# A transformer kernel on one NeuronCore: the key transposes placed ahead of the scores in each group of short TensorE steps

## Chip, cores and metric

The kernel runs on one core of one Trainium2 chip, as a single program. The metric is the device time of one execution in microseconds (us), lower is better.

## What is computed

Two layers of a perceiver-like model over 8 samples of 32 tokens, with a context of 512 rows of 512 numbers for each sample. Each layer has a cross attention, a second token mixer and a feed-forward part. The change touches the cross attention, which both layers have. Cut to what matters (layer 0; layer 1 has no latent keys, so 512 keys rather than 544, and adds a mask):

```python
kv = jnp.concatenate([context, latents], axis=1)
q = (latents @ Wq).reshape(bsz, q_len, HEADS, HEAD_DIM).transpose(0, 2, 1, 3)
k = (kv @ Wk).reshape(bsz, kv_len, KV_HEADS, HEAD_DIM).transpose(0, 2, 1, 3)
v = (kv @ Wv).reshape(bsz, kv_len, KV_HEADS, HEAD_DIM).transpose(0, 2, 1, 3)
q = rms_norm(q, q_norm_w)
k = rms_norm(k, k_norm_w)
scores = jnp.einsum('bhgqd,bhkd->bhgqk', qg, k) * scale
probs = jax.nn.softmax(scores.astype(jnp.float32), axis=-1).astype(q.dtype)
out = jnp.einsum('bhgqk,bhkd->bhgqd', probs, v)
return out @ Wo
```

There are 32 query heads and 8 key heads of 128, so four query heads of 32 tokens (128 rows) share one key head.

## The kernel before

**Tiling.** A unit is one sample with four of the eight key heads (`UNIT_H`); there are 16 units in a layer (`UNITS`). A unit's keys and values are made from its context in two quads, `side` 0 and 1, so there are 32 quads in a layer (`PAIRS`), numbered `m = 2 * u + side`. A quad makes two key tiles (`kn`, each 128 keys by four heads) and two value tiles by seven half-size products of 6 matmuls (p1 to p7, line 1736, run by `mm3`, lines 54 to 56). Each product is in a split form: three matmuls for one, of a rounded part and a rest.

**A key tile's way.** ScalarE copies a product to `kn` (line 1947 for the tile of parity 0, 1997 for parity 1), VectorE adds the other product to tile 0 (2126), ScalarE squares (1928), VectorE sums the squares (2101), GpSimd takes the root (1674, 1677), VectorE multiplies `kn` by it (2107: "normalise", it increments `k_normed`). Then TensorE transposes the tile in four steps to the bank `g_ktbank` (`kt`, lines 1794 to 1800), ScalarE takes the rounded part to `kT_hi` (1896) and VectorE the rest (2052, it increments `kt_lo`).

**A head's way.** `score` (lines 1741 to 1761): the head's queries against the four transposed key tiles, into the bank `g_sbank`; three matmuls of 512 columns in layer 1, six of 272 in layer 0. VectorE takes the maximum (2070 in layer 0, 2075 in layer 1), ScalarE the exponential (1909), VectorE the inverse of the sum (2061), ScalarE scales (1916). `p_transpose` (1763 to 1773) transposes the result `p` to `g_pobanks` in four steps, with one more for the latent keys in layer 0 (1769). ScalarE copies it to `pT` (1923), and `pv` (1775 to 1792) multiplies with the values, 8 recorded matmuls, in layer 0 with one more for the latent keys (1790, whose operand VectorE makes in lines 2084 to 2087).

**Order.** Nothing schedules the program: each engine's list is written out by hand, and engines wait for each other's semaphores. TensorE's list for a quad is `quad` in lines 1802 to 1858. Between the products stand two groups of short steps. The first (lines 1829 to 1833) comes after p2, and transposes the key tile of parity 1 of the quad before, `kt(2 * m - 1, 1)`; the second (1846 to 1850) comes after p5's place in the list, and transposes the tile of parity 0 of this quad, `kt(2 * m, 0)`. In each group the transposes of one head's `p`, the scores of a later head and the values' product of the first stand around it. In quads 0 to 2 (`early`) the first tile is transposed later, and in unit 0 the second one.

GpSimd's list for a quad (1705 to 1720) takes the root for the tile of the quad before; on side 1 the split of the next queries follows directly (`split_queries`, 1688 and 1692).

Of the kernel before, what the change touches and what calls it, by code (L numbers as in the profile page):

```python
# [44 lines left out]
def need(eng, sem, value):  # L45

    if isinstance(value, int) and value <= 0:
        return
    eng.wait_ge(sem, value)


def mm3(nc, out, a, b, start, stop, reopen=False):

    nc.tensor.matmul(out, a[0], b[1], start=start, stop=False, skip_group_check=reopen)  # L54
    nc.tensor.matmul(out, a[0], b[0], start=False, stop=False, skip_group_check=reopen)  # L55
    return nc.tensor.matmul(out, a[1], b[0], start=False, stop=stop, skip_group_check=reopen)  # L56
# [272 lines left out]
def is_at(i, value):  # L329

    return isinstance(i, int) and i == value
# [1083 lines left out]
def attend(layer, ctx, banks, border, follow=None, then=None):  # L1415
# [95 lines left out]
    def kept(m, name):  # L1511

        return len(COPIES) * m + COPIES.index(name) + 1

    def prepared(hf, m):

        return tail and hf == 0 and not is_at(m, PAIRS // 2)
# [26 lines left out]
    def early(m):  # L1544

        return is_at(m, 0) or is_at(m, 1) or is_at(m, 2)

    def exists(a):

        return not isinstance(a, int) or 0 <= a < UNIT_H * UNITS  # L1550

    def scored(u, par, side, second):

        if second:
            return UNIT_H * (u - 1) + 2 * side, u - 1, 1 - par, 2 * side
        if side:
            return UNIT_H * (u - 1) + 1, u - 1, 1 - par, 1
        return UNIT_H * (u - 2) + 3, u - 2, par, 3

    def summed_up(u, par, side, second):  # L1560

        if side:
            return UNIT_H * (u - 1) + int(second), u - 1, 1 - par, int(second)
        return UNIT_H * (u - 2) + 2 + int(second), u - 2, par, 2 + int(second)
# [166 lines left out]
    def tensor(pe):  # L1731
        def product(hf, side, left, right, bank, start):

            a, wt = context.block(side, left), kvw.block(hf, right)
            for c in range(DC // 2):
                last = mm3(nc, bank[:, :], tuple(h[:, c * P:(c + 1) * P] for h in a),
                           tuple(h[:, c * UW:(c + 1) * UW] for h in wt),
                           start and c == 0, c == DC // 2 - 1, not start)
            return last

        def score(a, u, apar, k):

            if not exists(a):
                return
            if k == 0:
                pe.wait_ge(kt_lo, CT * (u + 1))
                pe.wait_ge(q_lo, u + 1)
                if tail:
                    pe.wait_ge(kl_lo, u + 1)
            if tail:  # L1750
                need(pe, p_ready, a)
                for qp, kp in ((0, 1), (0, 0), (1, 0)):
                    for side in range(2):
                        last = nc.tensor.matmul(sbank[:, side * CTX:side * CTX + HALF], q[qp][:, apar, k, :],  # L1754
                                                kT[kp][:, apar, k, side * HALF:(side + 1) * HALF],
                                                start=(kp == 1), stop=(qp == 1))
            else:
                need(pe, m_done, a)
                last = mm3(nc, sbank[:, 0:CTX], tuple(h[:, apar, k, :] for h in q),
                           tuple(h[:, apar, k, :] for h in kT), True, True)  # L1760
            last.then_inc(s_done, 1)

        def p_transpose(a, free, value, bank):
            if not exists(a):
                return
            pe.wait_ge(p_scaled, a + 1)
            if tail:
                pe.wait_ge(free, value)
                nc.tensor.transpose(bank[0:SEQ, 0:P], p[:, CTX:KEYS], ident[:]).then_inc(tail_turned, 1)
            need(pe, pt_ready, a)  # L1770
            for t in range(CT):
                last = nc.tensor.transpose(ptbank[:, t * P:(t + 1) * P], p[:, t * P:(t + 1) * P], ident[:])  # L1772
            last.then_inc(pt_done, 1)

        def pv(a, u, apar, k, loads):

            if not exists(a):
                return
            if k == 0:
                pe.wait_ge(va_added, 2 * (u + 1))  # L1780
                if tail:
                    pe.wait_ge(vlat_loaded[apar], loads)
            pe.wait_ge(pt_ready, a + 1)
            need(pe, ot_ready, a)
            for t in range(CT):
                last = nc.tensor.matmul(obank[:, 0:P], v[:, apar, t, k * HD:(k + 1) * HD], pT[:, t, :],  # L1786
                                        start=(t == 0), stop=(t == CT - 1 and not tail))
            if tail:
                pe.wait_ge(tail_ready, a + 1)
                last = nc.tensor.matmul(obank[:, 0:P], vlat[:, apar, k * HD:(k + 1) * HD], pTs[:, :],  # L1790
                                        start=False, stop=True)
            last.then_inc(o_done, 1)

        def kt(n, k):
            pe.wait_ge(k_normed, n + 1)
            need(pe, kt_lo, n)
            for h in range(UNIT_H):
                last = nc.tensor.transpose(ktbank[:, h * P:(h + 1) * P],  # L1798
                                           kn[:, k, h * P:(h + 1) * P], ident[:])
            last.then_inc(kt_done, 1)  # L1800

        def quad(hf, j, b, par, cycle, u, side, m):
            x_bank, y_bank = kbank[side], kbank[1 - side]
            fresh = (is_at(u, 0) or is_at(u, TURN)) and side == 0
            loads = 48 * (cycle + par)

            def wait_context(i):
                if prepared(hf, m):
                    pe.wait_ge(context.lo_ready, 2 * m + i + 1)
                else:  # L1810
                    pe.wait_ge(context.fetched[side][i], 16 * (u - (TURN if tail else 0)) + 16)

            def wait_weights(i):
                if fresh:
                    kvw.wait_block(pe, hf, i)

            wait_context(0)
            wait_weights(kvw.B11)
            need(pe, ka_added, m)
            product(hf, side, context.A11, kvw.B11, x_bank, True).then_inc(products, 1)  # L1820
            if is_at(m, 0):
                border.turn(pe, 0)
            wait_weights(kvw.B21)
            need(pe, copied, len(COPIES) * m)
            product(hf, side, context.A12, kvw.B21, y_bank, True).then_inc(products, 1)
            if is_at(m, 0):
                border.turn(pe, 1)
            else:
                p_transpose(summed_up(u, par, side, False)[0], va_added, m, zbank)
                score(*scored(u, par, side, False))  # L1830
                if not early(m):
                    kt(2 * m - 1, 1)
                pv(*summed_up(u, par, side, False), loads)
            wait_weights(kvw.T2)
            pe.wait_ge(copied, kept(m, "p1"))
            product(hf, side, context.S2, kvw.T2, x_bank, False).then_inc(products, 1)
            if early(m) and not is_at(m, 0):
                kt(2 * m - 1, 1)
            wait_context(1)
            wait_weights(kvw.T1)  # L1840
            need(pe, va_added, m)
            product(hf, side, context.S1, kvw.T1, zbank, True).then_inc(products, 1)
            wait_weights(kvw.T3)
            pe.wait_ge(copied, kept(m, "u2"))
            product(hf, side, context.S3, kvw.T3, x_bank, False).then_inc(products, 1)
            p_transpose(summed_up(u, par, side, True)[0], ka_added, m + 1, y_bank)
            score(*scored(u, par, side, True))
            if not is_at(u, 0):
                kt(2 * m, 0)
            pv(*summed_up(u, par, side, True), loads)  # L1850
            wait_weights(kvw.T4)
            pe.wait_ge(copied, kept(m, "u3"))
            product(hf, side, context.A22, kvw.T4, x_bank, False).then_inc(products, 1)
            if is_at(u, 0):
                kt(2 * m, 0)
            wait_weights(kvw.B22)
            pe.wait_ge(vb_added, m + 1)
            product(hf, side, context.S4, kvw.B22, zbank, False).then_inc(products, 1)
# [1570 lines left out]
```

## Time and profile before

| What | Value |
|---|---|
| Median of 3 runs | 1445.07 us (1444.0 to 1445.44) |
| The profiled execution's own time | 1443.81 us |
| Its span in the profile | 1442.0 us |
| TensorE matmul busy | 1414.9 us (98%) |
| TensorE weight load busy (beside the matmuls) | 1193.5 us (83%) |
| VectorE busy | 1021.4 us (71%) |
| ScalarE busy | 844.8 us (59%) |
| GpSimd busy | 361.7 us (25%) |
| Mean granted TensorE clock | 0.999 of full speed |

The profile is of one execution. Its own time is 1.81 us over its span, which covers first to last instruction. Matmuls are pipelined: a record lasts longer than the step from it to the next, so that the start times say more than the durations. In the names, `c0a_` is the cross attention of layer 0 and `c1a_` that of layer 1; buffer numbers are left out. Layer 0's attention stands at about 90 to 615 us, layer 1's at about 790 to 1285 us.

### The profile page before, as it was taken

Reading aid. Unit: us, or ns where it says so; the run is one execution under the profiler, and the core shown is the slowest. Engines: PE = TensorE matmul, PEld = TensorE weight load, DVE = VectorE, ACT = ScalarE, POOL = GpSimd, SP = SyncE. Lnnn points to the kernel's source line nnn. Section 1 sums busy time; section 2 is a strip of 40 time slices with the busy share of each in tenths; the row PEclk is TensorE's granted clock in tenths of the full one; section 3 lists DMA queues with packets and bytes.
Section 4 is the critical chain, followed back from the end, with each engine's and each line's share of the span. In section 5 each row is a group of like instructions: output and inputs, shape, how many; then the busy total and the mean of one; then the engine's idle time right before and its main releaser. Section 6 shows DMA issues by size and latency. Waiting matters only on the chain.

```text
span 1442.0 us, 24186 instructions
## 1 busy us (share of the span) xinstructions
PE 1414.9 (98%) x7942; PEld 1193.5 (83%) x7942; DVE 1021.4 (71%) x1897; ACT 844.8 (59%) x1476; POOL 361.7 (25%) x542
## 2 busy tenths in 40 slices
PE   8999999999999999999999999999999999999998
PEld 6877888887888888889778788888888888887887
DVE  7988988887666667758668555556755656776765
ACT  5845666656555556736447455556755555773443
POOL 2323323232342424015233322222221212101000
PEclk9999999999999999999999999999999999999999
DMA  7565545566455455347155433335543334342342
GB/s 274 180 234 192 189 161 186 190 220 227 142 188 169 150 163 174 117 183 229 73 178 211 153 125 126 130 118 178 166 134 121 133 123 161 132 183 68 110 159 96
DMA packets 79677, 232.44 MB, mean 161 GB/s; under 512 B 17696, under 2 KB 34848, under 8 KB 72320
## 3 DMA queue, kind: packets, MB, share of 16 engines
q1 hardware_dynamic: 79584, 231.25, 47.1%
q8 instruction: 52, 0.85, 0.2%
q14 instruction: 41, 0.34, 0.1%
HBM read 191.77 MB, written 39.45 MB: 160 GB/s over the span
## 4 chain that ended last, share of the span: by engine, by line
PE 86%; DVE 7%; DMA 2%; ACT 2%; issue 2%; POOL 1%; SPq 0%; DVEq 0%; POOLq 0%; ACTq 0%
PE g_kbanks L54 12%; PE g_kbanks L56 12%; PE g_kbanks L55 12%; PE g_pobanks L1786 8%; PE g_vbank L54 5%; PE g_vbank L55 5%; PE g_vbank L56 5%; PE g_pobanks L1772 4%; PE g_ktbank L1798 3%; PE g_sbank L1754 3%; PE g_sbank L54 2%; PE g_sbank L56 2%; PE g_sbank L55 2%; PE g_pobanks L54 1%; PE g_pobanks L56 1%
## 5 line engine op out<-in xcount | busy, mean ns | idle before, releaser
L54 PE MATMUL g_kbanks<-c_wkv_r,c_cT_r 128*128 128x512 f32 x768 | 311.4, 405 | 4.4 <-ACT c0a_keep L1984 2.1
L56 PE MATMUL g_kbanks<-c_wkv_r,c_cT_r 128*128 128x512 f32 x768 | 302.8, 394 | 0.0
L55 PE MATMUL g_kbanks<-c_wkv_r,c_cT_r 128*128 128x512 f32 x768 | 301.9, 393 | 0.0
L54 PEld LDWEIGHTS g_kbanks<-c_wkv_r,c_cT_r 128*128 128x128 f32 x768 | 144.8, 189 | 35.1 <-DVE c_wkv_r L257 2.7
L56 PEld LDWEIGHTS g_kbanks<-c_wkv_r,c_cT_r 128*128 128x128 f32 x768 | 144.2, 188 | 32.9
L55 PEld LDWEIGHTS g_kbanks<-c_wkv_r,c_cT_r 128*128 128x128 f32 x768 | 144.8, 189 | 27.2
L54 PE MATMUL g_vbank<-c_wkv_r,c_cT_r 128*128 128x512 f32 x256 | 101.1, 395 | 0.0
L55 PE MATMUL g_vbank<-c_wkv_r,c_cT_r 128*128 128x512 f32 x256 | 100.7, 393 | 0.0
L56 PE MATMUL g_vbank<-c_wkv_r,c_cT_r 128*128 128x512 f32 x256 | 100.6, 393 | 0.0
L1674 POOL TENSOR_TENSOR c1a_ms<-c1a_ss,c_const 128x4 f32<-128x4 f32 x64 | 13.7, 214 | 346.3 <-DVE c1a_ss L2101 346.3
L2107 DVE TENSOR_TENSOR c1a_kn<-c1a_kn,c1a_rstd 128x512 f32<-128x512 f32 x64 | 66.7, 1042 | 43.1 <-POOL c1a_rstd L1677 43.1
L1674 POOL TENSOR_TENSOR c0a_ms<-c0a_ss,c_const 128x4 f32<-128x4 f32 x64 | 12.9, 201 | 325.7 <-DVE c0a_ss L2101 325.7
L1923 ACT ACTIVATE c1a_pT<-g_pobanks 128x512 f32<-128x512 f32 x64 | 38.2, 597 | 88.1 <-PE g_pobanks L1772 88.0
L2107 DVE TENSOR_TENSOR c0a_kn<-c0a_kn,c0a_rstd 128x512 f32<-128x512 f32 x64 | 61.4, 960 | 34.6 <-POOL c0a_rstd L1677 34.6
L1923 ACT ACTIVATE c0a_pT<-g_pobanks 128x512 f32<-128x512 f32 x64 | 38.1, 595 | 75.2 <-PE g_pobanks L1772 75.2
L2101 DVE TENSOR_REDUCE c1a_ss<-c1a_sq 128x4 f32<-128x512 f32 x64 | 43.8, 684 | 46.6 <-ACT c1a_sq L1928 46.4
L2075 DVE CUSTOM_DVE_ANT_0 c1a_sm<-g_sbank,c_mask 128x512 f32<-128x512 f32 x64 | 44.1, 688 | 45.3 <-issue 45.2
L1786 PE MATMUL g_pobanks<-c0a_pT,c0a_v 128*128 128x128 f32 x512 | 69.3, 279 | 4.2 <-ACT c0a_pT L1923 4.0
L1786 PEld LDWEIGHTS g_pobanks<-c0a_pT,c0a_v 128*128 128x128 f32 x512 | 63.3, 194 | 6.4 <-ACT c0a_pT L1923 5.8
L1786 PE MATMUL g_pobanks<-c1a_pT,c1a_v 128*128 128x128 f32 x512 | 67.7, 275 | 0.1
L1677 POOL TENSOR_TENSOR c0a_rstd<-c0a_ms,c_const 128x4 f32<-128x4 f32 x64 | 64.8, 1012 | 5.0
L1677 POOL TENSOR_TENSOR c1a_rstd<-c1a_ms,c_const 128x4 f32<-128x4 f32 x64 | 64.6, 1009 | 5.0
(541 smaller groups left out, 3776.2 us busy)
## 6 DMA issues: line engine op xcount, KB each, us to landing
c_cT_r<-ctx_split_dram SPq DMA_DIRECT2D x48, 1024.0 KB, 5.7
c_cT_r<-ctx_split_dram SPq DMA_DIRECT2D x48, 768.0 KB, 4.8
ctx_split_dram<-c_cT_r SPq DMA_DIRECT2D x16, 1792.0 KB, 6.5
c_wkv<-in_l_wo SPq DMA_DIRECT2D x16, 1024.0 KB, 4.9
g_stage<-in_l_wq SPq DMA_DIRECT2D x15, 1024.0 KB, 5.1
e_stage<-in_e_w SPq DMA_DIRECT2D x20, 768.0 KB, 4.2
c_cT<-in_ctx SPq DMA_DIRECT2D x32, 256.0 KB, 3.0
m_stage<-in_mix_ffn SPq DMA_DIRECT2D x10, 768.0 KB, 4.3
```

The lines of the kernel that those rows point to most:

```text
L54: nc.tensor.matmul(out, a[0], b[1], start=start, stop=False, skip_group_check=reopen)
L55: nc.tensor.matmul(out, a[0], b[0], start=False, stop=False, skip_group_check=reopen)
L56: return nc.tensor.matmul(out, a[1], b[0], start=False, stop=stop, skip_group_check=reopen)
L1677: nc.gpsimd.tensor_tensor(rstd[:, k, :], ms[:, k, :], const[:, 0, :], ALU.pow).then_inc(k_rstd, 1)
L1754: last = nc.tensor.matmul(sbank[:, side * CTX:side * CTX + HALF], q[qp][:, apar, k, :], kT[kp][:, apar, k, side * HALF:(side + 1) * HALF], ...
L1772: last = nc.tensor.transpose(ptbank[:, t * P:(t + 1) * P], p[:, t * P:(t + 1) * P], ident[:])
L1786: last = nc.tensor.matmul(obank[:, 0:P], v[:, apar, t, k * HD:(k + 1) * HD], pT[:, t, :], start=(t == 0), stop=(t == CT - 1 and not tail))
L1798: last = nc.tensor.transpose(ktbank[:, h * P:(h + 1) * P], kn[:, k, h * P:(h + 1) * P], ident[:])
L1923: nc.scalar.activation(pT[:, :, :], ptbank[:, :].rearrange("p (t n) -> p t n", t=CT), ACT.Copy).then_inc(pt_ready, 1)
L2075: nc.vector.tensor_tensor_reduce(out=sm[:], in0=sbank[:, 0:CTX], in1=mask[:], scale=-1.0, scalar=3.4e38, op0=ALU.add, op1=ALU.min, accum_o ...
L2101: nc.vector.tensor_reduce(ss[:, k, :], sq[:, :].rearrange("p (h d) -> p h d", h=UNIT_H), AX.X, ALU.add).then_inc(k_summed, 1)
L2107: nc.vector.tensor_tensor(heads, heads, rstd[:, k, :].unsqueeze(2).broadcast_to([P, UNIT_H, HD]), ALU.mult).then_inc(k_normed, 1)
```

## The change

In both groups of a quad the call of `kt` is put ahead of the call of `score`. Nothing is added or removed, and no other engine's list changes.

```diff
             else:
                 p_transpose(summed_up(u, par, side, False)[0], va_added, m, zbank)
-                score(*scored(u, par, side, False))
                 if not early(m):
                     kt(2 * m - 1, 1)
+                score(*scored(u, par, side, False))
                 pv(*summed_up(u, par, side, False), loads)
...
             p_transpose(summed_up(u, par, side, True)[0], ka_added, m + 1, y_bank)
-            score(*scored(u, par, side, True))
             if not is_at(u, 0):
                 kt(2 * m, 0)
+            score(*scored(u, par, side, True))
             pv(*summed_up(u, par, side, True), loads)
```

TensorE, layer 1, the first group of a quad, between two products into `g_kbanks`. `c1a_p` is a head's probabilities, `c1a_kn` the normalised key tile, `c1a_q` the queries of a head. Before:

```order
L56 MATMUL g_kbanks<-c_wkv_r,c_cT_r 128x512
L1772 MATMUL g_pobanks<-g_ident,c1a_p 128x128 x4
L54 MATMUL g_sbank<-g_stage_r,c1a_q_hi 128x512
L55 MATMUL g_sbank<-c1a_kT_hi,c1a_q_hi 128x512
L56 MATMUL g_sbank<-c1a_kT_hi,c1a_q_lo 128x512
L1798 MATMUL g_ktbank<-g_ident,c1a_kn 128x128 x4
L1786 MATMUL g_pobanks<-c1a_pT,c1a_v 128x128 x4
```

And with the change:

```order
L56 MATMUL g_kbanks<-c_wkv_r,c_cT_r 128x512
L1772 MATMUL g_pobanks<-g_ident,c1a_p 128x128 x4
L1798 MATMUL g_ktbank<-g_ident,c1a_kn 128x128 x4
L54 MATMUL g_sbank<-g_stage_r,c1a_q_hi 128x512
L55 MATMUL g_sbank<-c1a_kT_hi,c1a_q_hi 128x512
L56 MATMUL g_sbank<-c1a_kT_hi,c1a_q_lo 128x512
L1786 MATMUL g_pobanks<-c1a_pT,c1a_v 128x128 x4
```

The four transposes of the key tile have moved up past three score matmuls, to directly behind the four transposes of `p`; what stands around the group is the same.

TensorE, layer 0, the second group of a quad (the difference, with the rows of the change marked +):

```order
 L1769 MATMUL g_kbanks<-g_ident,c0a_p 32x128
 L1772 MATMUL g_pobanks<-g_ident,c0a_p 128x128 x4
+L1798 MATMUL g_ktbank<-g_ident,c0a_kn 128x128 x4
 L1754 MATMUL g_sbank<-g_stage_r,c0a_q_hi 128x272 x2
 L1754 MATMUL g_sbank<-c0a_kT_hi,c0a_q_hi 128x272 x2
 L1754 MATMUL g_sbank<-c0a_kT_hi,c0a_q_lo 128x272 x2
-L1798 MATMUL g_ktbank<-g_ident,c0a_kn 128x128 x4
 L1786 MATMUL g_pobanks<-c0a_pT,c0a_v 128x128 x4
```

Here they have moved past six score matmuls; nine transposes now stand in a row.

## Rows read from the trace of the kernel before

**Rows 1.** The page: busy time, and TensorE's granted clock in 40 slices

```profile
PE 1414.9 (98%) x7942; PEld 1193.5 (83%) x7942; DVE 1021.4 (71%) x1897; ACT 844.8 (59%) x1476; POOL 361.7 (25%) x542
...
PEclk9999999999999999999999999999999999999999
```

**Rows 2.** Waits of PE: us in total, times, longest us

```profile
PE g_ktbank L1798 <- DVE c1a_kn L2107: 0.8, 2, 0.6
```

**Rows 3.** Timeline, layer 1, first group on side 1, PE: start us, us, then the instruction

```profile
914.13 0.60 PE L1772 MATMUL g_pobanks<-g_ident,c1a_p 128*128 128x128 f32 x4
...
915.27 0.60 PE L1798 MATMUL g_ktbank<-g_ident,c1a_kn 128*128 128x128 f32 x4
915.71 1.06 PE L1786 MATMUL g_pobanks<-c1a_pT,c1a_v 128*128 128x128 f32 x8
```

**Rows 4.** Timeline, the same group, POOL and DVE

```profile
913.54 0.61 POOL L1688 CAST c1a_q_hi<-c_qT 128x512 fp32r x1
...
913.62 1.08 DVE L2107 TENSOR_TENSOR c1a_kn<-c1a_kn,c1a_rstd 128x512 f32<-128x512 f32 x1 [0.80 <-POOL c1a_rstd L1677]
```

**Rows 5.** Timeline, layer 1, quad 3, first group, where the transposes wait today

```profile
826.73 1.08 DVE L2107 TENSOR_TENSOR c1a_kn<-c1a_kn,c1a_rstd 128x512 f32<-128x512 f32 x1 [0.87 <-POOL c1a_rstd L1677]
...
828.35 1.06 PE L1786 MATMUL g_pobanks<-c1a_pT,c1a_v 128*128 128x128 f32 x8
```

**Rows 6.** Timeline, layer 1, first group on side 1 in a later unit

```profile
971.92 1.08 DVE L2107 TENSOR_TENSOR c1a_kn<-c1a_kn,c1a_rstd 128x512 f32<-128x512 f32 x1 [0.86 <-POOL c1a_rstd L1677]
...
972.38 0.60 PE L1772 MATMUL g_pobanks<-g_ident,c1a_p 128*128 128x128 f32 x4
```

**Rows 7.** Timeline, layer 1: first group on side 0; then normalise and start of a second group

```profile
928.17 0.69 DVE L2107 TENSOR_TENSOR c1a_kn<-c1a_kn,c1a_rstd 128x512 f32<-128x512 f32 x1 [0.80 <-POOL c1a_rstd L1677]
...
928.70 0.60 PE L1772 MATMUL g_pobanks<-g_ident,c1a_p 128*128 128x128 f32 x4
...
918.17 1.78 DVE L2107 TENSOR_TENSOR c1a_kn<-c1a_kn,c1a_rstd 128x512 f32<-128x512 f32 x1 [0.51 <-POOL c1a_rstd L1677]
...
920.74 0.60 PE L1772 MATMUL g_pobanks<-g_ident,c1a_p 128*128 128x128 f32 x4
```

**Rows 8.** Timeline, layer 1, quad 2, second group

```profile
818.93 0.39 PE L54 MATMUL g_sbank<-g_stage_r,c1a_q_hi 128*128 128x512 f32 x1
...
819.98 0.66 PE L1798 MATMUL g_ktbank<-g_ident,c1a_kn 128*128 128x128 f32 x4 [0.20 <-DVE c1a_kn L2107]
820.39 0.47 PE L54 MATMUL g_kbanks<-c_wkv_r,c_cT_r 128*128 128x512 f32 x1
```

**Rows 9.** Timeline, layer 0, second half, first group on side 1

```profile
442.28 1.08 DVE L2107 TENSOR_TENSOR c0a_kn<-c0a_kn,c0a_rstd 128x512 f32<-128x512 f32 x1 [0.80 <-POOL c0a_rstd L1677]
...
442.89 0.27 PE L1769 MATMUL g_vbank<-g_ident,c0a_p 128*32 128x128 f32 x1
...
445.44 0.30 PE L1790 MATMUL g_pobanks<-c0a_pT_stack,c_vlat 96*128 96x128 f32 x1
```

**Rows 10.** Timeline, layer 0, first half, second group on side 1

```profile
196.70 0.96 DVE L2107 TENSOR_TENSOR c0a_kn<-c0a_kn,c0a_rstd 128x512 f32<-128x512 f32 x1
...
196.76 0.27 PE L1769 MATMUL g_kbanks<-g_ident,c0a_p 128*32 128x128 f32 x1
...
199.60 0.31 PE L1790 MATMUL g_pobanks<-c0a_pT_stack,c_vlat 96*128 96x128 f32 x1
```

**Rows 11.** Timeline, layer 1, ACT: end of an exponential, and the copy after it

```profile
902.46 0.19 ACT L1909 ACTIVATION_READ_ACCUMULATOR c1a_p<-c1a_sm,c1a_nmax 128x1 f32 x1
903.63 0.60 ACT L1965 ACTIVATE c1a_keep<-g_kbanks 128x512 f32<-128x512 f32 x1 [0.99 <-PE g_kbanks L56]
...
909.14 0.19 ACT L1909 ACTIVATION_READ_ACCUMULATOR c1a_p<-c1a_sm,c1a_nmax 128x1 f32 x1
910.23 0.60 ACT L1997 ACTIVATE c1a_kn<-g_kbanks 128x512 f32<-128x512 f32 x1 [0.90 <-PE g_kbanks L56]
```

**Rows 12.** Timeline, layer 0, the change of weights, PE

```profile
326.78 1.99 PE L1786 MATMUL g_pobanks<-c0a_pT,c0a_v 128*128 128x128 f32 x8 [4.03 <-ACT c0a_pT L1923]
```

## The prediction

> **What bounds the kernel now.** I read the page first [rows 1]: TensorE is busy for 98% of the span at a granted clock of nine tenths or more in all 40 slices, and VectorE, the next, for 71%. So what counts is whether the change adds or removes time in TensorE's own row of instructions; a delay elsewhere counts only when TensorE comes to wait for it. The waits of TensorE say how often that happens at the key transposes: in layer 1 twice, 0.8 us in all [rows 2]. Then I read the timeline of single groups, since a wait of 0.2 us that may arise in each group is in no total of before.
>
> A group in the steady part of layer 1 runs without a gap [rows 3]. From the start of one four-step transpose to what follows it is 915.71 - 915.27 = 0.44 us. The transposes of the key tile start 915.27 - 914.13 = 1.14 us behind the group's start; 0.44 of that are the transposes of `p`, 0.70 the three score matmuls. That 0.70 is the only slack that the change takes away: it moves the key transposes to 0.44 behind the group's start.
>
> **Part 1: TensorE's own work.** Same instructions, same neighbours in kind: a run of transposes, then rounded-form matmuls, then the values' product. Eight transposes stand in a row now, each with a weight load of its own; eight values' matmuls do so already, at 0.44 us for four transposes and about the same for four of them, without a gap [rows 3]. I cost the order itself at 0.
>
> **Part 2: the new wait.** The key transposes need the normalised tile (line 2107). In the first group of a side-1 quad VectorE starts it at 913.62 and ends at 914.70 [rows 4]: it takes 1.08 us because GpSimd splits the queries at the same time (913.54 to 914.15); on side 0 the same instruction takes 0.69 [rows 7]. The new place of the transposes is 914.13 + 0.44 = 914.57, so they wait. What a wait costs I take from a group where they wait today [rows 5]: the tile is ready at 826.73 + 1.08 = 827.81, the instruction behind the transposes starts at 828.35, 0.54 later. Undisturbed that is 0.44; 0.10 goes for starting again.
>
> - Side 1, first group: the scores would start at 914.70 + 0.54 = 915.24 instead of 914.57 + 0.44 = 915.01: **+0.23**. Eight groups look like this one. Six look like that of [rows 6]: 971.92 + 1.08 + 0.54 = 973.54 against 972.38 + 0.88 = 973.26: **+0.28**. Sum 8 x 0.23 + 6 x 0.28 = 3.5 us. The normalise waits for GpSimd's root, whose chain begins with the copy of the last key product of the quad before. TensorE makes that product, so the chain moves along with TensorE and the wait returns in every unit. Nothing behind it gives it back, since TensorE has no other wait here.
> - Side 0, first group: ready at 928.17 + 0.69 = 928.86, plus 0.54 = 929.40 against 928.70 + 0.88 = 929.58 [rows 7]: 0, with 0.18 to spare. In two units, at the change of weights and at the end, other VectorE work is in front of it; I estimate 0.25 each, as above: 0.5 us.
> - Second groups of layer 1: the longest normalise starts at 918.17 and takes 1.78, to 919.95 [rows 7]; its group starts at 920.74 and would need it at 920.74 + 0.44 - 0.10 = 921.08: 0.
> - Start of layer 1: in quad 2's second group and quad 3's first the transposes wait already, and the three score matmuls run inside that wait [rows 5, 8]. With the transposes in front, the scores come after the wait: 2 x 0.70 = 1.4 us.
> - Layer 0, second half: ready at 442.28 + 1.08 = 443.36, plus 0.54 = 443.90, against 442.89 + 0.11 (the step for the latent keys, an estimate: a quarter of 0.44) + 0.88 = 443.88 [rows 9]: 0.02, in others up to 0.1. Nine groups, 0.5 us together.
> - Layer 0, first half: VectorE is full, and before the second group of side 1 the tile is ready only at 196.70 + 0.96 = 197.66 [rows 10]. The wait would be 197.66 + 0.54 - (196.76 + 0.99) = 0.45. But the last step of that group waits already: the product of the latent keys starts at 199.60, 2.84 behind the group's start, against 445.44 - 442.89 = 2.55 undisturbed [rows 9]. So 0.45 - 0.29 = 0.16 is left, in six groups; in some of them that step is later still. I take 0.5 us for the six, bounds 0 and 6 x 0.45 = 2.7. First groups here: 0.3. Quad 2, where scores ran inside a wait, has another wait right behind: 0.1, at most 0.7.
> - The change of weights in layer 0 holds TensorE for 4.03 us whatever stands in front of it [rows 12]: what the two groups before it lose is not counted.
>
> Sum: 3.5 + 0.5 + 1.4 + 0.5 + 0.5 + 0.3 + 0.1 = **6.8 us**.
>
> **Part 3: scores 0.44 us later** (0.67 where there is a wait too). Behind them stand maximum, exponential, inverse, scaling, then the next group's transposes of `p`. The cover is ScalarE's idle time: the exponential's last piece ends at 902.46 + 0.19 = 902.65 and the copy after it starts at 903.63, and 909.33 against 910.23 in the other group [rows 11]. Both copies are tied to TensorE's products. So 0.98 and 0.90 us cover 0.67 and 0.44: cost 0. If that cover were gone, the scaling would be late next and hold the next group's first step. The earlier transposes let ScalarE take the rounded key part sooner, which nobody waits for: gain 0.
>
> **The time.** 1443.81 (profiled execution; span 1442.0, 1.81 around it) + 6.8 = 1450.6. The median of the runs is 1445.07, 1.26 above that execution, so the forecast is 1445.07 + 6.8 = **1451.9 us**. A difference of 0.2% (2.9 us) is about what a measurement of this kernel tells from none.
>
> **Rivals.**
> 1. *The wait is paid once.* If the normalise hangs on something that doesn't follow TensorE, TensorE falls behind once by 0.23 us and finds every later tile ready. For it: what holds the normalise is POOL [rows 4]. Against: that chain begins with a copy of a TensorE product. Price 0.28 + 1.4 + about 1 in layer 0: +2.7, 1447.8 us. Chance 0.10.
> 2. *The late scores come through.* The cover of 0.98 us is used to 0.67, and in layer 0's first half VectorE is full, so a later maximum can push what stands behind it, the next normalise first. From that point each such group costs what is over: 14 groups of 0.3 us, or the six of 0.45 unabsorbed (2.7 instead of 0.5), +2 to +6 more: about 1456 us. Chance 0.14.
> 3. *Faster.* The key tile's transposed parts are ready 0.7 us sooner on ScalarE and VectorE. If it is that work which holds up `pT` or the stack in layer 0's first half, the existing 0.29 us waits [rows 10] go, in six groups, and with them perhaps as much again where they are longer: -1.7 to -3.5. It decides only if the normalise there ends before the transposes' new place, and it ends 0.35 us behind it. 1441.6 to 1443.4 us; chance 0.03.
> 4. *The clock.* All slices stand at full clock [rows 1]; after the 4.03 us wait the eight values' matmuls took 1.99 us instead of 1.06 [rows 3, 12], TensorE at the lower of its levels, 1.2 instead of 2.4 GHz. If a longer run of transposes brought that on, each group would pay 0.9 us or more: 118 groups, over 100 us. Chance 0.01. The Trainium skill, TensorE: Matmul & The Clock Gate, Part 4 (PE-mode transpose) says that transposes don't count as activity for the clock gate, which speaks against this change, since it puts them side by side. By that rule nothing need happen either, for the share of transposes is the same.
>
> **How the numbers follow.** The forecast's case has 0.72. Its own bounds: without the 0.10 for starting again (17 groups) and without layer 0's small terms it is +3.7, 1448.8; with layer 0's first half unabsorbed and the others at their upper bounds +10, 1455. The range of 8 in 10 takes in part of rivals 1 and 2: 1447.5 to 1456.5. Faster by over 0.2%: rival 3 in part, 0.03. Within 0.2%: most of rival 1 and the edge of the forecast, 0.11. Slower: 0.86.
>
> **What would show it.** In the waits of TensorE the key transposes on the normalised tile must rise from a few instances to some 25 or more, 0.1 to 0.3 us each (the idle part shown may be less, since records overlap). In a first group of side 1 in layer 1 the key transposes must start about 0.6 us behind the group's start, just behind the end of the normalise, instead of 1.14, and groups of side 0 must be as long as before. The distance from one such group to the same group of the next unit must grow by 0.23 to 0.28 us. The forecast is wrong if side-1 groups keep their length, if second groups in layer 1 show a wait, or if TensorE waits for `p` anywhere new.

## The result, and the profile after

The changed kernel takes **1450.94 us** (median of five runs, 1450.72 to 1452.15) against 1445.07 us before (1443.79 to 1446.39, in the same session): ratio 1.0044, 95% interval 1.003 to 1.0059. That is slower by 5.9 us, and the whole interval lies above 0.2%. The forecast was 1451.9 us. The profiled execution took 1450.72 us, with a span of 1448.9 us and a mean granted clock of 0.999.

The page, busy time and granted clock in 40 slices, as in [rows 1]:

```profile
PE 1418.8 (98%) x7942; PEld 1195.2 (82%) x7942; DVE 1021.9 (71%) x1897; ACT 846.1 (58%) x1476; POOL 361.7 (25%) x542
...
PEclk9999999999999999999999999999999999999999
```

The counts of instructions are the same, the clock too; the span is 6.9 us longer. The page shows nothing else, for the loss is many pieces of 0.1 to 0.45 us. The waits of PE (us in total, times, longest us), beside [rows 2]; layer 0's line stood at 1.9, 3, 0.7 before:

```profile
PEld g_ktbank L1798 <- DVE c1a_kn L2107: 4.2, 11, 1.3
...
PE g_ktbank L1798 <- DVE c0a_kn L2107: 3.4, 8, 1.4
...
PEld g_ktbank L1798 <- issue: 2.5, 8, 0.3
...
PE g_ktbank L1798 <- DVE c1a_kn L2107: 1.1, 2, 0.9
```

The matmul rows of layer 1 still count two instances, though 16 groups there have become longer. The rows of the weight loads (PEld) count them: 11 in layer 1 where it was 3 before, another 8 that the profile puts down to "issue" where there were none, and in layer 0 11 (6.8 us in all) where it was 3. One of the longer groups, first group on side 1, from the timeline (start us, us, instruction; compare [rows 3, 4]):

```profile
887.21 0.61 POOL L1688 CAST c1a_q_hi<-c_qT 128x512 fp32r x1
...
887.29 1.08 DVE L2107 TENSOR_TENSOR c1a_kn<-c1a_kn,c1a_rstd 128x512 f32<-128x512 f32 x1 [0.80 <-POOL c1a_rstd L1677]
...
887.82 0.60 PE L1772 MATMUL g_pobanks<-g_ident,c1a_p 128*128 128x128 f32 x4
...
888.50 0.42 PEld L1798 LDWEIGHTS g_ktbank<-g_ident,c1a_kn 128*128 128x128 f32 x4 [0.31 <-issue]
888.50 0.65 PE L1798 MATMUL g_ktbank<-g_ident,c1a_kn 128*128 128x128 f32 x4
...
888.91 0.47 PE L54 MATMUL g_sbank<-g_stage_r,c1a_q_hi 128*128 128x512 f32 x1
...
889.68 1.05 PE L1786 MATMUL g_pobanks<-c1a_pT,c1a_v 128*128 128x128 f32 x8
```

The normalised tile is ready at 887.29 + 1.08 = 888.37, 0.55 behind the group's start, and the key transposes start at 888.50, at +0.68. The same group on side 0:

```profile
902.11 0.69 DVE L2107 TENSOR_TENSOR c1a_kn<-c1a_kn,c1a_rstd 128x512 f32<-128x512 f32 x1 [0.80 <-POOL c1a_rstd L1677]
...
902.61 0.60 PE L1772 MATMUL g_pobanks<-g_ident,c1a_p 128*128 128x128 f32 x4
...
903.05 0.60 PE L1798 MATMUL g_ktbank<-g_ident,c1a_kn 128*128 128x128 f32 x4
...
903.41 0.48 PE L54 MATMUL g_sbank<-g_stage_r,c1a_q_hi 128*128 128x512 f32 x1
...
904.18 1.05 PE L1786 MATMUL g_pobanks<-c1a_pT,c1a_v 128*128 128x128 f32 x8
```

Here the tile is ready at +0.19, the transposes start at +0.44, the scores at +0.80, the values at +1.57. On side 1 the values start at 889.68 - 887.82 = +1.86: 0.29 later. Second groups look like this one.

**Where the 6.9 us are.** I set each group's length in the two traces side by side, and read the length of layer 1's attention from its first key transposes to its last values' product: 1280.53 - 798.05 = 482.48 us before, 1287.37 - 800.04 = 487.33 after, +4.85.

| Piece | Predicted | In the trace after |
|---|---|---|
| Layer 1, side 1, first groups, 14 | 3.5 | 14 x 0.285 = 4.0 |
| Layer 1, other first groups that wait | 0.5 | 0.2 (one group; the other is in the next line but one) |
| Start of layer 1 | 1.4 | 0.7 |
| Scores that come too late: twice at the change of weights (0.26, 0.37), once at the last unit (0.45) | 0 | 1.1 |
| Products between the groups of layer 1 | 0 | -1.1 |
| Layer 0, second half, 8 groups | 0.5 | 0.8 |
| Layer 0, first half: first groups; second groups; quad 2 | 0.3; 0.5; 0.1 | 1.0; 0.0; 0.0 |
| Sum | 6.8 | 6.7 |

The products' -1.1 is not measured by itself: it is what is left of the 4.85; it fits the units, which grew by 0.19 each where their one waiting group grew by 0.285. The sum agrees better than its terms: misses of up to 1.1 us either way cancel. Of layer 0's part, some 0.2 goes in the wait at the change of weights, and the instant at which layer 1 starts isn't sharp: in a later run whose program is the old one up to there it was 799.96 against 798.05. So for layer 0 only the groups' lengths count, and for layer 1 the length above.

The start of layer 1, quad 2's second group and quad 3's first, PE and DVE, beside [rows 5, 8]:

```profile
821.22 0.69 DVE L2107 TENSOR_TENSOR c1a_kn<-c1a_kn,c1a_rstd 128x512 f32<-128x512 f32 x1 [0.87 <-POOL c1a_rstd L1677]
...
821.97 0.66 PE L1798 MATMUL g_ktbank<-g_ident,c1a_kn 128*128 128x128 f32 x4 [0.88 <-DVE c1a_kn L2107]
822.38 0.47 PE L54 MATMUL g_sbank<-g_stage_r,c1a_q_hi 128*128 128x512 f32 x1
...
824.12 0.69 DVE L2159 TENSOR_TENSOR c1a_v<-g_vbank,c1a_keep 128x512 f32<-128x512 f32 x1
...
824.86 0.50 PE L54 MATMUL g_vbank<-c_wkv_r,c_cT_r 128*128 128x512 f32 x1 [0.17 <-DVE c1a_v L2159]
...
828.72 1.08 DVE L2107 TENSOR_TENSOR c1a_kn<-c1a_kn,c1a_rstd 128x512 f32<-128x512 f32 x1 [0.87 <-POOL c1a_rstd L1677]
...
829.08 0.60 PE L1772 MATMUL g_pobanks<-g_ident,c1a_p 128*128 128x128 f32 x4
...
829.86 0.66 PE L1798 MATMUL g_ktbank<-g_ident,c1a_kn 128*128 128x128 f32 x4 [0.17 <-DVE c1a_kn L2107]
```

In the first of the two the three scores now come behind the wait: from the key transposes to the next product it is 1.18 us where it was 820.39 - 819.98 = 0.41, so 0.77 is lost, as forecast. Between the two groups another 0.37 goes, and this is late scores too: the sum for a value tile (line 2159) stands behind the scores' maximum in VectorE's list, ends at 824.81, and a product waits for it. Before, it ended at 821.27, and no wait shows. But the next tile is ready at 829.80 - 829.08 = +0.72 of the second group, where before it was at 827.81 - 825.95 = +1.86. That group is 2.77 us long instead of 3.22: the 0.70 that I had added there is a gain of 0.45, and the three make 0.69. The wait there is paid once.

The late scores, PE and DVE at the change of weights in layer 1 (line 257 makes the rest of the new weights):

```profile
1021.96 0.69 DVE L2075 CUSTOM_DVE_ANT_0 c1a_sm<-g_sbank,c_mask 128x512 f32<-128x512 f32 x1
...
1022.57 1.22 DVE L257 TENSOR_TENSOR c_wkv_r<-c_wkv,c_wkv_r 128x1024 fp32r<-128x1024 f32 x1
...
1025.16 1.21 DVE L257 TENSOR_TENSOR c_wkv_r<-c_wkv,c_wkv_r 128x1024 fp32r<-128x1024 f32 x1
...
1026.43 0.50 PE L54 MATMUL g_kbanks<-c_wkv_r,c_cT_r 128*128 128x512 f32 x1 [0.55 <-DVE c_wkv_r L257]
```

Before, the wait shown there was 0.18. The maximum (2075) waits for the scores, and the weights stand behind it in VectorE's list. In the last unit it is the next sample's context (line 536):

```profile
1253.36 1.28 DVE L536 TENSOR_TENSOR c_cT_r<-c_qT,c_cT_r 128x512 fp32r<-128x512 f32 x2
...
1254.15 0.47 PE L54 MATMUL g_kbanks<-c_wkv_r,c_cT_r 128*128 128x512 f32 x1 [0.53 <-DVE c_cT_r L536]
```

### The profile page after: what moved, and what is told of

Its sections match the earlier page's. It is cut to its first block, busy times and chain, and to the rows that moved or that the text cites. A ratio compares the mean times of both kernels' runs of the same rounds, so it can differ in the third digit from the quotient of the medians.

```text
span 1448.9 us, 24186 instructions
## 1 busy us (share of the span) xinstructions
PE 1418.8 (98%) x7942; PEld 1195.2 (82%) x7942; DVE 1021.9 (71%) x1897; ACT 846.1 (58%) x1476; POOL 361.7 (25%) x542
## 4 chain that ended last, share of the span: by engine, by line
PE 84%; DVE 9%; ACT 2%; DMA 2%; issue 2%; POOL 1%; SPq 0%; DVEq 0%; POOLq 0%; ACTq 0%
PE g_kbanks L54 12%; PE g_kbanks L56 11%; PE g_kbanks L55 11%; PE g_pobanks L1786 7%; PE g_vbank L54 5%; PE g_vbank L56 5%; PE g_vbank L55 5%; PE g_ktbank L1798 4%; PE g_pobanks L1772 3%; PE g_sbank L1754 3%; PE g_sbank L54 2%; PE g_sbank L56 2%; PE g_sbank L55 2%; PE g_pobanks L54 1%; DMA g_stage<-in_l_wq 1%
## 5 line engine op out<-in xcount | busy, mean ns | idle before, releaser
L1786 PEld LDWEIGHTS g_pobanks<-c1a_pT,c1a_v 128*128 128x128 f32 x512 | 66.8, 191 | 5.9 <-ACT c1a_pT L1923 0.6
```

## Experiments

Theory A is the prediction's: the loss is the wait of the key transposes for the normalised tile, in first groups on side 1. B: transposes side by side, or the order itself, cost something. C: the scores, 0.44 us later, hold something in each group. Each kernel was timed beside the kernel before on the same chip. The control is the kernel before where nothing else is said. "Length" is that of layer 1's attention as above (482.5 before, 487.3 with the change), "unit" the distance of a first group on side 1 to the next in the first half of layer 1 (914.13 - 885.01 = 29.12 before; 887.82 - 858.51 = 29.31 with the change).

| Run | us | Ratio to before, 95% | Length | Unit |
|---|---|---|---|---|
| 1 side 1's first groups in the old order | 1446.90 | 1.0003 to 1.0021 | 483.1 | 29.05 |
| 2 change, queries split later | 1447.37 | 1.0005 to 1.0023 | 482.7 | 29.03 |
| 3 before, queries split later | 1445.08 | 0.999 to 1.0008 | 481.0 | 29.04 |
| 4 first groups only | 1449.49 | 1.0024 to 1.0052 | 487.4 | 29.37 |
| 5 second groups only | 1445.99 | 0.9995 to 1.0013 | 481.9 | 29.03 |
| 6 behind one score matmul | 1446.20 | 0.9995 to 1.0013 | 483.6 | 29.10 |
| 7 change, late root on side 0 | 1471.58 | 1.0167 to 1.0195 | 498.0 | 30.1 |
| 8 before, late root on side 0 | 1447.05 | 1.0004 to 1.0022 | 482.7 | 29.13 |
| 9 two places in the old order | 1450.18 | 1.0024 to 1.0051 | 486.2 | 29.32 |
| 10 new order where it is free | 1444.49 | 0.9987 to 1.0005 | 481.3 | 29.03 |

**1. Side 1's first groups in the old order**

```diff
+                if side:
+                    score(*scored(u, par, side, False))
                 if not early(m):
                     kt(2 * m - 1, 1)
-                score(*scored(u, par, side, False))
+                if not side:
+                    score(*scored(u, par, side, False))
```

> The first groups of side-1 quads keep the old order (scores, then key transposes); all other groups have the new one. Theory A (the key transposes of those groups wait for the normalise, 0.285 us a unit in layer 1 and 0.1 in layer 0): what is left is the start of layer 1 (0.7) and layer 0's first half (up to 0.7): 1446 to 1446.7 us, 0.7 to 1.5 over before. Theory B (the run of eight or nine transposes costs by itself, the same in each of some 118 groups): a quarter of 5.9 goes, 1449.5. Theory C (the later scores come through): the same in three groups of four, 1449.5.

Measured 1446.9, 1.6 over the kernel before: 4.3 of the 5.9 us are gone with a quarter of the groups, though three quarters keep eight transposes in a row and late scores. It lies 0.2 above the range that A gave and 2.6 below what B and C gave, so these two fall as causes of the bulk.

**2 and 3. The wait taken away, the order kept.** The normalise on side 1 takes 1.08 us, not 0.69, because GpSimd casts the queries beside it. An idle power on GpSimd (an instruction of 128 by 4 numbers whose result nobody reads, 1.01 us) holds the cast back; run 3 is the control, the same in the kernel before.

```diff
             if side == 1:
+                nc.gpsimd.tensor_tensor(idle[:, :], const[:, 1, :], const[:, 0, :], ALU.pow)
                 split_queries(u, par, 2 * m, is_at(m, 1))
```

> The order of the change in all groups; on GpSimd an idle power of 128x4 numbers into a scratch tile, about 1.0 us, stands ahead of the split of the queries on side 1, so that the split doesn't run beside the normalise of the key tile. Theory A: that normalise takes 0.69 instead of 1.08 us and ends about 0.2 behind the group's start, the wait in side-1 first groups goes, and 4.2 us in layer 1 and 0.7 to 1.2 in layer 0 with it: 1446 to 1447 us. Theories B and C: it stays at 1451, since TensorE's order and the scores' place are those of the change.

> Control for the run with the delayed split: the same idle GpSimd instruction in the kernel before. All theories: the normalise is 0.69 us here too, but nobody waits for it; 1445 us, within 0.5 of before.

Run 2, first group on side 1, POOL, DVE and PE:

```profile
856.86 1.01 POOL L1714 TENSOR_TENSOR c1a_idle<-c_const 128x4 f32<-128x4 f32 x1
856.93 0.69 DVE L2109 TENSOR_TENSOR c1a_kn<-c1a_kn,c1a_rstd 128x512 f32<-128x512 f32 x1 [0.80 <-POOL c1a_rstd L1678]
...
857.45 0.60 PE L1774 MATMUL g_pobanks<-g_ident,c1a_p 128*128 128x128 f32 x4
857.82 0.61 POOL L1689 CAST c1a_q_hi<-c_qT 128x512 fp32r x1
857.89 0.60 PE L1800 MATMUL g_ktbank<-g_ident,c1a_kn 128*128 128x128 f32 x4
...
859.02 1.05 PE L1788 MATMUL g_pobanks<-c1a_pT,c1a_v 128*128 128x128 f32 x8
```

The normalise takes 0.69, is ready at +0.17, and the transposes start at +0.44: no wait, and the values at +1.57 as on side 0. All 118 groups have the new order here, and the loss falls from 5.9 to 2.1 us (1447.37 against 1445.31), or 2.3 beside its control, run 3. That is 0.4 above the range of theory A and far below the 1451 of B and C. Beside run 3 the length is 1.7 us more, with units as long (29.03 and 29.04): what is left in layer 1 is no cost of each group. The expectation had left out the late scores, 1.1 us in the table above. Part of the 2.1 is the granted clock of single executions: those of the kernel before took 1444.6 us in the mean at 0.999 (11 of 27) and 1446.1 at 0.996 (6), and at 0.998 run 2 (six executions) stands 0.9 over it (five). This separates the wait from the order most sharply. What holds the tile is also shown: a cast on GpSimd beside it, not VectorE's own queue.

**4 and 5. Each kind of group alone.** The new order in first groups only, and in second groups only:

```diff
-                score(*scored(u, par, side, False))
                 if not early(m):
                     kt(2 * m - 1, 1)
+                score(*scored(u, par, side, False))
```

> The new order in first groups alone, second groups as before. Theory A: nearly the whole loss is there: layer 1's 14 waits of 0.285 (4.0), the change of weights in layer 1 (0.6), layer 0 about 1.2: 5.2 to 6 us over before, 1450.3 to 1451. Theory B: half the groups, half the loss, 1448. Theory C: half of it as well, 1448.

> The key transposes lead only in the second group of each quad; first groups as before. A (they wait for the normalised tile, and only in first groups on side 1): left are the 0.4 to 0.7 us at the start of layer 1 and the second groups of layer 0's first half (+0.07 in three of them, the others 0): 1445.8 to 1446.5 us, and a steady unit of layer 1 is as long as before. B (eight transposes in a row cost something themselves, as often here as in first groups) or C (scores 0.44 later hold something): half of the loss, 1448 us or more.

First groups alone lose 4.2 us, second groups 0.5, which can't be told from nothing. Run 4 came out 0.8 below the expectation, run 5 within it. B and C had forecast 1448 for each. In the traces the parting is as clear: run 4 has the whole length of the change (487.4 against 487.3), run 5 none of what was added.

**6. Behind one score matmul** (in layer 0 behind two of six). `score` takes a function that it calls behind its first matmul:

```diff
+                nc.tensor.matmul(sbank[:, 0:CTX], hi, klo, start=True, stop=False)
+                if between:
+                    between()
+                nc.tensor.matmul(sbank[:, 0:CTX], hi, khi, start=False, stop=False)
```

> In both groups the key transposes stand behind the first of the three score matmuls in layer 1 (behind the first two of six in layer 0), so 0.23 to 0.26 us later than with the change. A: in first groups on side 1 of layer 1 the tile is ready at +0.55, TensorE can start on it at +0.68, and the place is at +0.67: a wait of 0.02 to 0.05 in 14 groups, under 1 us; in layer 0 nothing; at the start of layer 1 0.5 at most. 1446 to 1447 us. B (transposes side by side, or the break in the order): the transposes no longer stand side by side, so nothing or the same +5.9 if any departure from the old order costs. C (last score matmul 0.44 late, as with the change): 1450 or more.

First group on side 1, DVE and PE:

```profile
856.70 1.07 DVE L2114 TENSOR_TENSOR c1a_kn<-c1a_kn,c1a_rstd 128x512 f32<-128x512 f32 x1 [0.80 <-POOL c1a_rstd L1677]
...
857.22 0.60 PE L1781 MATMUL g_pobanks<-g_ident,c1a_p 128*128 128x128 f32 x4
857.58 0.48 PE L1765 MATMUL g_sbank<-g_stage_r,c1a_q_hi 128*128 128x512 f32 x1
...
857.91 0.65 PE L1807 MATMUL g_ktbank<-g_ident,c1a_kn 128*128 128x128 f32 x4
...
858.86 1.05 PE L1795 MATMUL g_pobanks<-c1a_pT,c1a_v 128*128 128x128 f32 x8
```

One score matmul ahead is nearly enough: the transposes start at +0.69, 0.02 later than in a side-0 group of this run, and the values at +1.64 instead of +1.57. So a wait of 0.02 costs 0.07. The time is 1446.2 us, at the lower end of what A gives; the last score matmul is as late as with the change, for which C had forecast 1450 or more.

**7 and 8. The dose.** Does the slack of 0.70 us that the change takes away behave as such? The tile of side 0's first group is made late in both orders, by an idle power inside GpSimd's root:

```diff
             nc.gpsimd.tensor_tensor(ms[:, k, :], ss[:, k, :], const[:, 1, :],
                                     ALU.add).then_inc(k_mean, 1)
+            if late:
+                nc.gpsimd.tensor_tensor(idle[:, :], const[:, 1, :], const[:, 0, :], ALU.pow)
...
-                root(2 * m - 1, 1)
+                root(2 * m - 1, 1, side == 0)
```

> The change, and on side 0 an idle power of 128 by 4 (0.98 us on GpSimd) inside the root for the first group's tile, so that the normalised tile is ready about 0.98 us later there: at +1.16 in layer 1, +1.12 in layer 0. A: each of the 15 first groups on side 0 in each layer waits 0.13 more than that less 0.44 (0.55 in layer 0), 0.85 and 0.70 us: 12.8 + 10.5 = 23, so some 1474 us. If the wait were paid once for all: 1452. Against its control (the same delay in the old order) the difference is about 0.70 a group, the three score matmuls, 30 x 0.70 + 5.9 = 27 us. B or C: the order costs 5.9 with the delay as without it, so 5.9 over the control.

> Control for the run before it: the same idle power in the old order. The transposes stand at +1.14 in layer 1 and would be able to start at 1.16 + 0.13 = 1.29: 0.15 in 15 groups, 2.3 us; in layer 0 they stand at +1.30 and wait for nothing. 1447 to 1449 us by each theory, a few us more if VectorE, which is full in layer 0's first half, doesn't take a late normalise.

First group on side 0 in run 7, then in run 8, DVE and PE:

```profile
884.02 0.60 PE L1775 MATMUL g_pobanks<-g_ident,c1a_p 128*128 128x128 f32 x4
884.37 0.69 DVE L2110 TENSOR_TENSOR c1a_kn<-c1a_kn,c1a_rstd 128x512 f32<-128x512 f32 x1 [1.65 <-POOL c1a_rstd L1680]
...
885.19 0.65 PE L1801 MATMUL g_ktbank<-g_ident,c1a_kn 128*128 128x128 f32 x4 [0.57 <-DVE c1a_kn L2110]
```

```profile
872.25 0.60 PE L1775 MATMUL g_pobanks<-g_ident,c1a_p 128*128 128x128 f32 x4
872.60 0.69 DVE L2110 TENSOR_TENSOR c1a_kn<-c1a_kn,c1a_rstd 128x512 f32<-128x512 f32 x1 [1.65 <-POOL c1a_rstd L1680]
...
873.42 0.65 PE L1801 MATMUL g_ktbank<-g_ident,c1a_kn 128*128 128x128 f32 x4
```

The tile is ready at +1.04 in both. In the old order the transposes stand at +1.17, and the group is 0.09 longer than 2.38 us; in the new one it is 3.16, 0.78 longer. The same delay costs 1.6 us in the old order (1447.05 against 1445.47), and 24.5 more in the new. B and C had 5.9 there. Run 7 is 2.4 us below the expected 1474: the tile came 0.12 earlier than expected, and there are 14 such groups in a layer, where the expectation took 15. Against the change, layer 1's are longer by 0.77 or 0.78, two that waited there already by 0.39 and 0.55, 10.2 together; layer 0's by 0.43 to 0.70, 8.2 together. With the change's own 5.9 this makes 24.3, where 26.1 are measured; 1.8 us are not assigned. The wait is paid in every unit. It is the tile's readiness, with 0.13 to TensorE's start, less the place of the transposes: 1.04 + 0.13 - 0.44 = 0.73, and another 0.05.

**9. The two places of the late scores.** Theory D, formed on the trace after: the waits at the change of weights and in the last unit come of the scores, not of the key tile.

```diff
+                if not tail and is_at(m, 2 * TURN):
+                    score(*scored(u, par, side, False))
                 if not early(m):
                     kt(2 * m - 1, 1)
-                score(*scored(u, par, side, False))
+                if tail or not is_at(m, 2 * TURN):
+                    score(*scored(u, par, side, False))
```

The second group of quad 31 likewise.

> The change, with the old order kept in two of layer 1's 64 groups: the first group of quad 16, where the key and value weights change, and the second group of the last quad. After the first of them the changed kernel waits 0.37 longer for the rest of the new weights, and 0.26 longer for p inside the group; after the other 0.45 longer for the next sample's context. Theory D (there the scores, 0.44 us later, come through: VectorE takes the maximum later, and the weights' or the context's rest stands behind it in its list): both waits fall back, 0.8 to 1.1 us less, 1449.8 to 1450.1 us; the first product behind the last value product of the last quad's neighbour starts 0.45 after its forerunner, as before, and not 0.92. If these waits come from something else that the change brings: they stay, 1450.9 us.

```profile
1026.06 0.19 PEld L54 LDWEIGHTS g_kbanks<-c_wkv_r,c_cT_r 128*128 128x128 f32 x1 [0.36 <-DVE c_wkv_r L257]
```

The idle time ahead of this weight load was 0.60 before and 0.97 with the change, and is 0.36 now; from the first group to the next it is 1027.57 - 1020.14 = 7.43 us, 7.44 before and 8.07 with the change. In the last unit the product stands 0.44 behind its forerunner, 0.92 with the change. The length falls by 1.2 us. The time, 5.0 us over its kernel before where the change had 5.9, can't show it by itself; the trace does. One part stays: the group at 1020.14 is 3.01 us long, as with the change (2.75 before), and it was so in run 5, where it had the old order too. What comes late there is `pT`, from the second group ahead of it: ScalarE scales that group's `p` later, so that its copy of `pT` starts 1.46 behind the start of the group at 1019.88 with the change, 1.21 behind that at 1016.05 before. What is lost is saved at the wait for the weights.

Runs 4 and 5 part the two places as well. With first groups alone the stretch at the change of weights is 7.88 us and the last unit is as before. With second groups alone the stretch is 7.43, though its group is 3.01 long, and the last unit is 0.45 longer.

**10. The new order where it is free,** in second groups of units 2 to 14 of layer 1:

```diff
+            lead = not tail and not is_at(u, 0) and not is_at(u, 1) and not is_at(u, UNITS - 1)
+            if lead:
+                kt(2 * m, 0)
             score(*scored(u, par, side, True))
-            if not is_at(u, 0):
+            if not lead and not is_at(u, 0):
                 kt(2 * m, 0)
```

> The old order everywhere, but for the second groups of units 2 to 14 of layer 1, where no wait arises. A unit with the new order and without a wait was 29.03 us long in three runs, one of before 29.12. If that comes of the new order in second groups, 13 units give 1.2 us: 1444.2 us, which the times can hardly tell from no change; the unit's length in the trace tells it (29.03 against 29.12). If not, 1445.4 and 29.12.

1444.49 against 1445.17, ratio 0.9996 (0.9987 to 1.0005): no version that is shown to beat the kernel before. A unit is 29.03 us long, and the length is 1.2 us shorter. Run 3 warns against taking that for an effect of the order: it has the old one and units of 29.04. Why a unit is 0.08 us shorter in both stays open.

## Why the prediction was right

- **The mechanism.** Part 2 named the wait of side 1's first groups as the largest term, from one row's sum: ready at +0.57, place at +0.44. Runs 1, 2 and 4 show it from three sides. That it returns in every unit, since the chain to the normalise follows TensorE, holds: 14 groups in layer 1, and the dose of run 7. Rival 1 (paid once) was right for one spot, the start of layer 1.
- **Its size.** 0.23 was forecast for the eight groups, 0.285 measured in all 14. The step that failed is the undisturbed place of the scores: I took two runs of four transposes as 0.44 + 0.44 = 0.88, and the second run takes only 0.36 when matmuls on 512 columns follow it (scores at +0.80). The end of the sum was right: tile ready to next instruction was taken as 0.54, and it is 888.91 - 888.37 = 0.54. In groups like [rows 6] it is less (0.47), so that two errors of 0.07 and 0.08 cancel there and 0.28 held. That the sum of all pieces came out within 0.1 us of the forecast's 6.8 is luck too: the misses in the table are as large as 1.1.
- **Side 0 and second groups of layer 1** were costed at 0 and kept 2.38 us, but for the two first groups at and behind the change of weights.
- **The start of layer 1** was forecast at 1.4, twice the three scores, and came at 0.7. I took the two groups as independent; the first one's delay shortens the second one's wait, and 0.37 of the delay is late scores.
- **Part 3, late scores at 0,** failed in four spots: three of 1.1 us in all, and the 0.37 at the start of layer 1. I had read the cover on ScalarE in a steady group; where something that TensorE soon needs is queued behind the maximum on VectorE (new weights, the next sample's context, a value tile), up to 0.45 comes through. That is rival 2's mechanism, but at the singular places, not in layer 0's first half where I looked for it. Run 9 shows it for the 0.37 at the weights and the 0.45; run 4 for the 0.26 (that group is 2.74 long there, with the second groups in the old order). For the start of layer 1 it is read from the trace.
- **"In two units, at the change of weights and at the end", 0.5:** one group waits (+0.22, second unit behind the change). The group at the end belongs to `finish`, whose order isn't changed.
- **Layer 0.** Second half 0.8 instead of 0.5: eight groups of 0.1, by the same step as in "Its size" (scores at +0.90 undisturbed, not +0.99). First half: first groups 1.0 instead of 0.3, 0.39 of it in the one just before the weights change, which the forecast had left out because the wait of 4.03 us behind it would take it up (the wait moved along, and only some 0.2 came back); second groups 0 instead of 0.5. There three groups grew by 0.07 and three shrank by 0.09: the last step's wait took up the new one even more fully than the 0.29 I allowed.
- **Nothing behind it gives it back** was wrong by 1.1 us, if the table's line is right: the products of layer 1 took that much less. It isn't shown that the wait is what they gave back, for units without any wait came out 0.07 to 0.09 shorter than before too (runs 1, 2, 3, 5 and 10).
- **The clock.** 0.999 and nines in all slices, the upper of the two levels. So whatever the Trainium skill (TensorE: Matmul & The Clock Gate, Part 4) makes of transposes, their standing side by side didn't lower the clock here; their share is the same as before, so its rule isn't put to a test by this.
- **The signs.** The start of the key transposes "about 0.6 behind the group's start" came at +0.68 (+0.66 to +0.69 in the six groups like [rows 6]), and the groups of side 0 kept their length. "From a few instances to some 25 or more" in the waits of TensorE depends on the rows: those of the matmuls go from 5 to 10 in both layers and layer 1 still shows two, so they are a bad sign; those of the weight loads go from 6 to 30, with the 8 that stand at "issue". And a unit grew by 0.19, not by 0.23 to 0.28, though its group grew by 0.285.

## To carry to other kernels

On an engine that is never idle, a step that needs another engine's result should stand as late in a group as its own readers allow; work that is ready anyway belongs in front of it. Where the slack is enough, the order costs nothing that could be told here (runs 5 and 10). Read the slack as (place of the step) - (end of what it needs), for each kind of group apart, since the same instruction on VectorE ended 0.4 us later on side 1 only for what ran beside it on GpSimd. And when a step moves back by 0.4 us, look for its cover at the exceptional places (first quads, change of weights, last unit), not in the steady group.

## What the runs showed of the hardware

- **A short wait costs more than it lasts.** A wait that held the transposes by 0.02 (run 6) made the group 0.07 longer, and in the changed kernel a start 0.24 late (+0.68 for +0.44) made it 0.285 longer: some 0.05 more. Runs 7 and 8 show the same at other lengths: 0.73 late and 0.78 longer, 0.03 late and 0.09 longer. The 0.05 comes beside the time from the tile's end to TensorE's start, 0.13 us in eight of the 14 groups and 0.06 in the six like that of [rows 6].
- **A VectorE instruction on 128x512 depends on GpSimd beside it:** 0.69 us with a small power beside it, 1.08 with the cast, 1.78 with the difference of the same size (second groups on side 1, [rows 7]). Holding the cast back by 0.96 gave the 0.69 on side 1 as well. The 1.78 was not tested by a run of its own; in the trace of before the two stand side by side, 918.11 to 919.41 and 918.17 to 919.95:

```profile
918.11 1.30 POOL L1692 TENSOR_TENSOR c1a_q_lo<-c_qT,c1a_q_hi 128x512 fp32r<-128x512 f32 x1
```

- **Thousandths of the granted clock show in the time:** in the 27 executions of the kernel before beside runs 1 to 4, 1444.6 us at a mean of 0.999, 1445.3 at 0.998, 1446.1 at 0.996. The two go together; no run sets the clock apart.
- **TensorE's products aren't of fixed length:** a unit without any visible wait took 29.12 us before, and 29.03 to 29.05 in runs 1, 2, 3, 5 and 10, with the same instructions on TensorE. The groups are within 0.01 us of 2.38 in all of them, so most of it lies in the products between. No run here tells why.
